# A recurrence with a mixture of experts behind it on one core: moving shared half units out of the recurrence, pairing reciprocal roots on VectorE, and two banks in turn for the later units

## The reference, cut to what matters

```python
# layer 1
xn = layernorm(x, ln_w, ln_b)
u = xn @ Ws.T + bs + xn @ Wi.T + bi          # 16 states
h_t = tanh(h_{t-1} @ A.T + u_t)              # 256 steps in order
out = (H @ Wo.T + bo) * sigmoid(xn @ Wg.T + bg) + x
x = layernorm(x + out)
# layer 2, T = 8192 tokens, E = 8 experts, top 2 of them
scores = softmax(x @ gate_w.T)
idx = top_k(scores + gate_b, 2); rw = scores at idx
h = silu((x @ w1 + b1) * (x @ w3 + b3))      # per expert, width 176
y = sum over the two experts of rw * (h @ w2 + b2)
z = the same with one shared expert for all tokens
x = layernorm(x + y + z)
```

## Time and profile before

| What | us |
|---|---|
| median of three runs | 517.06 |
| lowest, highest | 516.9, 523.76 |
| the profiled execution | 517.55 |
| its span (first to last instruction) | 515.8 |

### The profile page before, as it was taken

How to read it: one execution, slowest core, us unless ns; L and a number is a source line. 1 busy time by engine, 2 the same in 40 slices (tenths; PEclk the granted TensorE clock), 3 DMA queues, 4 the chain that set the end, 5 groups by cost and what they waited for, 6 DMA issues and landing times.

```text
span 515.8 us, 11180 instructions
## 1 busy us (share of the span) xinstructions
PE 451.1 (87%) x2842; PEld 353.6 (69%) x2842; DVE 347.0 (67%) x1562; ACT 336.7 (65%) x870; POOL 302.0 (59%) x331
## 2 busy tenths in 40 slices
PE   5879999999999988877898996899999998988691
PEld 3546766666666665666897875788888887777350
DVE  5454589898888989665757782345544568778772
ACT  3645777777777775464575764557677777777454
POOL 4100003777776775575677777777666577777232
PEclk9978999999999999799998998889999999999886
DMA  3663112333333222596465675567666588882472
GB/s 111 132 230 113 54 37 84 97 95 99 93 93 95 77 80 74 151 259 193 135 177 145 182 204 165 159 197 215 208 182 197 176 268 251 285 283 84 163 245 102
DMA packets 58228, 79.81 MB, mean 155 GB/s; under 512 B 11182, under 2 KB 37803, under 8 KB 58166
## 3 DMA queue, kind: packets, MB, share of 16 engines
q1 hardware_dynamic: 49516, 62.17, 41.7%
q0 software_dynamic: 8640, 16.93, 9.5%
q10 hardware_dynamic: 10, 0.00, 0.0%
HBM read 47.85 MB, written 25.84 MB: 143 GB/s over the span
## 4 chain that ended last, share of the span: by engine, by line
PE 48%; DVE 20%; issue 10%; POOL 9%; ACT 8%; SPq 2%; DMA 2%; ACTq 0%; DVEq 0%; POOLq 0%
PE py L1292 7%; PE p L1275 6%; PE py L1293 5%; PE pu L1347 5%; PE p L1280 5%; PE ph L1285 5%; POOL ys L585 4%; POOL xs L578 4%; PE pt L1429 2%; DVE z L1083 2%; PE pm L1406 2%; ACT hT L659 2%; DVE z L1078 2%; PE pu L1234 2%; ACT t3b L643 1%
## 5 line engine op out<-in xcount | busy, mean ns | idle before, releaser
L585 POOL DMA_INDIRECT ys<-yp,xp x142 | 145.0, 1021 | 58.6 <-issue 36.0
L578 POOL DMA_INDIRECT xs<-x,place_i x128 | 124.7, 974 | 58.9 <-issue 22.7
L659 ACT ACTIVATE hT<-pu,bu 16x32 f32<-16x32 f32 x256 | 78.7, 308 | 61.3 <-PE pu L1347 56.2
L650 ACT ACTIVATE hid<-z 128x512 f32<-128x512 f32 x103 | 64.7, 628 | 65.8 <-DVE z L1083 65.2
L1347 PEld LDWEIGHTS pu<-hT,aT 128*66 128x66 f32 x512 | 54.4, 141 | 58.0 <-ACT hT L659 52.9
L1347 PE MATMUL pu<-hT,aT 128*66 128x32 f32 x512 | 78.6, 241 | 11.9 <-ACT hT L659 11.7
L1078 DVE SCALAR_TENSOR_TENSOR z<-p,wp,t3a 128x256 f32<-128x256 f32 x71 | 34.3, 483 | 61.1 <-ACT t3a L638 54.5
L1292 PE MATMUL py<-wp,hid 128*128 128x128 f32 x284 | 59.2, 290 | 12.4 <-DVE yp L1104 9.7
L1292 PEld LDWEIGHTS py<-wp,hid 128*128 128x128 f32 x284 | 45.0, 192 | 27.9 <-DVE yp L1104 19.5
L1293 PE MATMUL py<-wp,hid 128*128 128x128 f32 x284 | 55.4, 277 | 0.0
L566 POOL TENSOR_TENSOR rstd_in<-ve_in,neghalf 128x4 f32<-128x4 f32 x16 | 16.4, 1027 | 66.3 <-DVE ve_in L793 66.2
(11 more groups left out here) (272 smaller groups left out, 969.7 us busy)
## 6 DMA issues: line engine op xcount, KB each, us to landing
wp<-packed SPq DMA_DIRECT2D x71, 320.0 KB, 3.4
xp<-xs SPq DMA_DIRECT2D x71, 130.0 KB, 2.9
weights<-ys SPq DMA_DIRECT2D x16, 512.0 KB, 4.7
xt<-in_L_attn_x SPq DMA_DIRECT2D x16, 256.0 KB, 3.1
x<-x SPq DMA_DIRECT2D x16, 256.0 KB, 2.7
packed<-weights SPq DMA_DIRECT2D x1, 2560.0 KB, 8.6
ys<-yp,xp POOLq DMA_INDIRECT x142
yb<-x SPq DMA_DIRECT2D x16, 128.0 KB, 2.7
```

The lines of the kernel that those rows point to most:

```text
L578: g.indirect_dma_start(out=xs[:, :], out_offset=bass.IndirectOffsetOnAxis(ap=place_i[b % NB][:, c, t * Q + q:t * Q + q + 1], axis=0), in_= ...
L585: g.indirect_dma_start(out=ys[:, :], out_offset=bass.IndirectOffsetOnAxis(ap=xp[j % NX][:, h, DEST:DEST + 1].bitcast(int32), axis=0), in_= ...
L650: nc.scalar.activation(hid[u % NH][:, :], z[u % 2][:, :], ACT.Silu).then_inc(hid_ready, 1)
L659: nc.scalar.activation(hT[k % 2][0:N, c], pu[k % 2][0:N, c], ACT.Tanh, bias=bu[:, 0:1]).then_inc(h_ready, 1)
```

## The change

The first halves of tiles 8 to 12 no longer run in the recurrence: `KEPT` = 8 tiles keep theirs there, and tiles 8 to 15 have both halves among the dense units, one shared half after every two pages (`BETWEEN` = 2) instead of three. For these tiles the transposed halves are kept in `yb` of the tile, and the DMA into `yb` is not made; both halves of the result take the tile's own rows from `x1`. At the places in the recurrence where the five units had their up and down matmuls (`w3a`, `w1a`, `wb`, `down`, `down_too`), TensorE does four dummy matmuls each, ahead of the step's own matmul.

The input roots of tiles 4 to 15 ride with the middle roots of the tiles four earlier: the two share buffers (`ve_two`, `rstd_two`), and the Newton instructions work on 8 values instead of 4. The input statistics lie three places later. GpSimd keeps the input roots of tiles 0 to 3.

Units from place 280 (`SWITCH`) to the last page use, in turn, `p1`, `p3`, `py` and, as second banks, `pu0`, `pu1`, `pm`; `ph` and `pt` stay single.

By the layout's rules the dense units are then 71 pages and 24 halves, places 250 to 344, the sums start 7 places later (`SUM_AT` of tile 0 goes from 319 to 326), and the whole count ends at 385 instead of 378.

```diff
-    AT = dict(load=-56, in_stats=-44, in_rstd=-42, ...
+    AT = dict(load=-56, in_stats=-41, in_rstd=-38, ...
+    SWITCH = 280
-    APART, FILL, AFTER, BETWEEN = 0, 0, 3, 3
+    KEPT, AFTER, BETWEEN = 8, 3, 2
     def lay_out_units():
-        start = {at("shared", k): ("shared", k, 0) for k in range(TILES) if at("shared", k) < PAGES_FROM - 8}
-        kept = [("shared", k, 1) for k in range(TILES)]
-        kept += [("shared", k, 0) for k in range(TILES) if ("shared", k, 0) not in start.values()]
...
+        start = {at("shared", k): ("shared", k, 0) for k in range(KEPT)}
+        kept = [("shared", k, 1) for k in range(KEPT)]
+        kept += [("shared", k, h) for k in range(KEPT, TILES) for h in range(HALF)]
...
+    TWO_BANKS = [u for u, unit in enumerate(UNITS) if SWITCH <= unit[0] <= UNITS[UNIT_OF_PAGE[sum(PAGES) - 1]][0]]
+    SECOND = set(TWO_BANKS[1::2])
+    def before_in_bank(u):
+        return max([v for v in range(u) if (v in SECOND) == (u in SECOND)], default=-1)
...
+        ve_two, rstd_two = ([sb(f"{w}_two{i}", [P, 2, Q]) for i in range(2)] for w in ("ve", "rstd"))
+    p1s, p3s, pys = (p1, pu[0]), (p3, pu[1]), (py, pm)
+        def of_unit(banks, u):
+            return banks[u in SECOND]
...
         def on_pool(w, turn):
-            return turn - SOON if w == "out" else turn
+            return turn - SOON if w == "out" else turn if turn < LEAD else -1
         def x1T_half(k, h):
+            if k >= KEPT:
+                return yb[k][:, h * HALF:(h + 1) * HALF, :].rearrange("p q d -> p (q d)")
+        QUIET = {at("shared", k) + SPARSE[what] for k in range(KEPT, TILES) for what in ("w3a", "w1a", "wb", "down", "down_too")}
+        QUIET = {n for n in QUIET if n < PAGES_FROM}
...
-                    if k >= APART:
+                    if k < KEPT:
                         sp.dma_start(yb[k][:, HALF:Q, :], x1_rows(k, 0)[:, HALF:Q, :]).then_inc(half_kept[k % NE], 16)
...
-                if k is not None:
+                if k is not None and k < LEAD:
                     rsqrt("in", k)
...
             def newton(w, k, part):
+                two = w == "mid" and k + LEAD < TILES
+                if two:
+                    y, ve_ = (t[i][:, :, :].rearrange("p n q -> p (n q)") for t in (rstd_two, ve_two))
...
+                    if two:
+                        v.wait_ge(ve_ready["in"], k + LEAD + 1)
+                        v.wait_ge(normed["in"], k + LEAD - NORMS["in"] + 1)
...
             def up_w3(u):
-                wait(pe, t3a_ready, u)
-                nc.tensor.matmul(p3[:, 0:PAGE], ...
+                bank_left(u)
+                wait(pe, t3a_ready, before_in_bank(u) + 1)
+                nc.tensor.matmul(of_unit(p3s, u)[:, 0:PAGE], ...
             def up_w1(u):
-                wait(pe, za_ready, u)
+                wait(pe, za_ready, before_in_bank(u) + 1)
             def down(u, h):
-                wait(pe, evacuated, u)
+                wait(pe, evacuated, before_in_bank(u) + 1)
...
             for n in range(BEGIN, END):
                 if n < first_down:
                     hold_clock(IDLE.get(n, 0) if n < 0 else 2 if n < 16 else 1)
+                if n in QUIET:
+                    pe.wait_ge(za_ready, KEPT)
+                    hold_clock(4, p1)
```

More of the change, by code:

```diff
@@ L110, in lay_out_units @@
     def lay_out_units():
-        start = {at("shared", k): ("shared", k, 0) for k in range(TILES) if at("shared", k) < PAGES_FROM - 8}
-        kept = [("shared", k, 1) for k in range(TILES)]
-        kept += [("shared", k, 0) for k in range(TILES) if ("shared", k, 0) not in start.values()]
-        for i, unit in enumerate(kept[:FILL]):
-            start[PAGES_FROM - FILL + i] = unit
-        among, behind = kept[FILL:len(kept) - AFTER], kept[len(kept) - AFTER:]
+        start = {at("shared", k): ("shared", k, 0) for k in range(KEPT)}
+        kept = [("shared", k, 1) for k in range(KEPT)]
+        kept += [("shared", k, h) for k in range(KEPT, TILES) for h in range(HALF)]
+        among, behind = kept[:len(kept) - AFTER], kept[len(kept) - AFTER:]
         n = PAGES_FROM
@@ L260, in rnn_gate_moe_block @@
         primer = sb("primer", [P, Q])
[L261 removed]
+        root_a, root_b = ({w: sb(f"root_{c}_{w}", [P, 2 * Q]) for w in ("mid", "out")} for c in "ab")
         tri_f, tri = sb("tri_f", [P, P]), sb("tri", [P, P], bf16)
@@ L292, in rnn_gate_moe_block @@
         x1 = sb("x1", [P, NE * 2 * Q, ROW])
-        x1T = [[sb(f"x1T{h}_{i}", [D, PAGE]) for i in range(n)] for h, n in enumerate((NS, TILES))]
+        x1T = [[sb(f"x1T{h}_{i}", [D, PAGE]) for i in range(n)] for h, n in enumerate((NS, KEPT))]
         yb = [sb(f"yb{k}", [P, Q, D]) for k in range(TILES)]
@@ L298, in rnn_gate_moe_block @@
         mv = {w: [sb(f"mv_{w}{i}", [P, Q, 2]) for i in range(NORMS[w])] for w in NORMS}
-        ve = {w: [sb(f"ve_{w}{i}", [P, Q]) for i in range(NORMS[w])] for w in NORMS}
-        rstd = {w: [sb(f"rstd_{w}{i}", [P, Q]) for i in range(NORMS[w])] for w in NORMS}
+        ve_two, rstd_two = ([sb(f"{w}_two{i}", [P, 2, Q]) for i in range(2)] for w in ("ve", "rstd"))
+        ve, rstd = ({"mid": [t[:, 0, :] for t in two], "in": [t[:, 1, :] for t in two],
+                     "out": [sb(f"{w}_out{i}", [P, Q]) for i in range(NORMS["out"])]} for w, two in (("ve", ve_two), ("rstd", rstd_two)))
         shift = {w: [sb(f"shift_{w}{i}", [P, Q]) for i in range(NORMS[w])] for w in NORMS}
@@ L682, in _ @@
                         act.wait_ge(x1T_ps, k + 1)
-                        if k >= NS and h == 0:
+                        if NS <= k < KEPT and h == 0:
                             act.wait_ge(lg_ps, k - NS + 1)
@@ L797, in scale @@
                 i = turn % NORMS[w]
-                if on_pool(w, turn) < 0:
+                if on_pool(w, turn) < 0 and w == "in":
+                    v.wait_ge(root_step["mid"], ROOT * (turn - LEAD + 1))
+                elif on_pool(w, turn) < 0:
                     v.wait_ge(root_step[w], ROOT * (turn + 1))
@@ L807, in newton @@
                 i = k % NORMS[w]
-                y, ve_, a, b = rstd[w][i][:, :], ve[w][i][:, :], root_a[w][:, :], root_b[w][:, :]
+                two = w == "mid" and k + LEAD < TILES
+                if two:
+                    y, ve_ = (t[i][:, :, :].rearrange("p n q -> p (n q)") for t in (rstd_two, ve_two))
+                else:
+                    y, ve_ = rstd[w][i][:, :], ve[w][i][:, :]
+                a, b = (t[w][:, 0:2 * Q if two else Q] for t in (root_a, root_b))
                 def then(step):
@@ L1093, in result @@
                     qs = slice(half * HALF, (half + 1) * HALF)
-                    if half == 1 and k >= APART:
-                        v.wait_ge(half_kept[k % NE], 16 * kept_of(k))
+                    if half == 1 and k < KEPT:
+                        v.wait_ge(half_kept[k % NE], 16)
                         own = yb[k][:, qs, :]
@@ L1262, in unit_of, with bank_left @@
                 return wp[a % NW][:, :], xpT[a % NP][:, :]
+            def bank_left(u):
+                if u == min(SECOND):
+                    pe.wait_ge(v_ready, TILES)
+                    pe.wait_ge(lg_ready, TILES)
+                    pe.wait_ge(x1T_ready, TILES)
+                    pe.wait_ge(place_ready, len(GROUPS))
+                    pe.wait_ge(table_step, TABLE + 1)
             def up_w3(u):
@@ L1314, in late_bank_free, with hold_clock @@
                 wait(pe, place_ready, sum(routed("rank", b) < n for b in range(len(GROUPS))))
-            def hold_clock(times):
+            def hold_clock(times, bank=py):
                 for _ in range(times):
-                    nc.tensor.matmul(py[:, 0:PAGE], ones[:, :], ones[:, :].unsqueeze(1).to_broadcast([P, HALF, P]), start=True, stop=True)
+                    nc.tensor.matmul(bank[:, 0:PAGE], ones[:, :], ones[:, :].unsqueeze(1).to_broadcast([P, HALF, P]), start=True, stop=True)
             def last_sum(k):
```

29 lines of the change are left out of this document (12 added, 17 removed).

## The result

| Four runs each | us |
|---|---|
| before: median (lowest, highest) | 517.03 (516.9, 523.76) |
| after: median (lowest, highest) | 536.27 (533.97, 539.07) |
| ratio, 95% interval | 1.0362 (1.0327 to 1.0397) |
| profiled execution after, its span | 533.97, 532.2 |

The changed kernel is 3.6% slower. The forecast was 521.6 with a range to 529. The profiled execution is the fastest of the four, so its trace shows 16.4 us of span more, and the median is another 2.3 above it. The slower executions have the lower clock: TensorE's mean granted clock is 0.940 in the fastest, then 0.934, 0.933 and 0.924 in the slowest; in the profiled execution of the kernel before it is 0.955.

What follows compares the result with a forecast made beforehand. It took the step chain, then GpSimd's scatters, then the ScalarE-VectorE loop as bounds. 1.0 - 6.3 - 2.3 + 12.1 + 0 = +4.5 us on the profiled 517.55 gave 522.05, 521.6 as a median; range 511 to 529.

Steps and rivals of the forecast that it cites:

- The recurrence: 256-step chain: dummy matmuls cost 3.8 us, VectorE's relief gives back 2.8; net +1.0 us, bounds -3 to +4.
- VectorE's stalls: TensorE's waits for a late VectorE in tiles 11 to 14, 2.8 us, were all taken as gone.
- The input roots: Moving 12 of 16 input roots from GpSimd to wider VectorE instructions changes nothing: 0, bounds -1 to +1 us.
- GpSimd's stretch: Scatter stretch from 249.48 to 332 us: two pages fewer, -5.1 us, and an earlier start, -1.2; in all -6.3.
- I take the middle, -1.2: The start of GpSimd's stretch could move by -3.6 to +1.2 us; -1.2 was taken.
- rival 3: Beginning of the pages costs more: page 2 waits for the transposer, no refill saving or VectorE relief; 529 us, chance 0.15.
- The refill: After VectorE's wait for a scatter at 335.99 us, a second bank brings the next `hid` sooner: -2.3 us, once.
- the steady loop: Dense units after the refill: the banks give nothing, periods stay 2.52 and 2.25 us.
- Rival 1: The banks shorten the dense units' loop to 2.41 and 2.19 us: -10.1 us, 511.5 us in all, chance 0.15.
- More units: Behind place 284, three more pages and two more halves cost +12.1 us; one normalizing pair fewer among the units, -1.5.
- Rival 4: The moved units cost nothing, hidden under GpSimd's work: 514.8 us; chance 0.2 together with another rival.
- The sums: Sums at the end: -1.5 us inside the units, +1.5 in the tail, 0 in total; bounds -2 to +3.

Runs made afterwards that it cites:

- e8: The changed kernel without the dummy matmuls that stand in for the moved units; 540.32 us, ratio 1.0407 to the kernel before.
- e9: The changed kernel with eight dummy matmuls in each place instead of four; 537.27 us, ratio 1.0369 to the kernel before.
- e7: The kernel before with the input-root change alone; 519.28 us, ratio 1.0027.
- e16: The changed kernel with shared halves at places 253, 256 and every third place on; 529.43 us, ratio 1.0207 to the kernel before.
- e6: The kernel before with the two banks alone; 515.40 us, ratio 0.9951.
- e18: The kernel before with shared halves at places 253, 257 and then every third place, one set of banks; 511.92 us, ratio 0.9881.
- e11: The kernel before with the two banks and shared halves at places 253, 257 and then every third place; 506.52 us, ratio 0.9794.
- e5: The changed kernel with shared halves at places 253, 257 and every third place from 260 on; 528.29 us, ratio 1.0226 to the kernel before.
- e3: The kernel before with the two banks alone, on a slow chip; 629.78 us against 626.80 for the kernel before there.
- e15: The kernel of e11 with shared halves at 253, 257 and every second place from 259 on; 508.50 us, ratio 0.9853 to the kernel before.

## Why the prediction was wrong

Three steps failed: that the granted clock stays as it is, that GpSimd has no pause once it has begun its stretch, and that the end of the program keeps its order.

**The recurrence (+1.0).** The step of the prediction that failed here is one that it doesn't name: it took TensorE's granted clock as unchanged. Its two terms were right where the clock was full. Four dummies against none make the step behind the logits 0.43 us longer (1.44 in the changed kernel, 1.01 in e8; forecast 0.44) and the step behind the transposes of `og` 0.31 (1.02 and 0.71; forecast 0.31); against the kernel before the first is 0.63 us longer (1.43 and 0.80), and what the other 0.2 are isn't known.

VectorE's stalls went as forecast: the waits for `og` of 0.38 and 1.31 us are gone in every kernel with moved units. In tiles 10 to 14 the steps that have no dummies take 45.2 us before and 42.2 in e9 at a clock of 1.00, but 45.5 in the changed kernel: so the clock costs 3.3 us there, and at the full clock the tiles would have taken about 63.8 us for the 64.1 before (an estimate: the 42.2 of e9 and the changed kernel's own 21.6 for the steps with dummies). The twelve steps from 239 to 251 take 13.4 us, against 11.1 in e9 and 11.0 before. So the units that left had done more than delay the chain; they had kept the clock up, and four dummies per place are too few: 0.93 and 0.74 instead of 1.00 and 0.87. (The edit also puts them at places 248 and 249, which I didn't count; the two steps take 0.4 us more.) Step 251 comes at 221.7 to 227.1 us in the four profiles with four dummies (mean 223.5) and at 214.7 to 217.9 in the six without moved units (mean 216.1). The term is +7.4 over these, +4.8 in the pair compared, and above my bound of +4 in both.

**The input roots (0).** e7 has +1.4 (0.1 to 2.7) where my bound was +1. Its profile reaches step 251 no later than the kernel before (215.8 and 217.1), so the recurrence doesn't lose it; where it is lost stays open.

**GpSimd's stretch (-6.3).** Two pages less are 5.1 us, and with the halves at 253 and 257 the stretch is 75.6 us instead of 81.2. In the changed kernel it is 78.7. The step that failed is the assumption that GpSimd has no pause once it has begun: it waits 3.31 us inside, for a page that slipped at a held place, and does so at any clock. "I take the middle, -1.2" for its start failed as well, with +1.6 from step 251; but that goes with the low clock and not with the held places, for e9, in the same order with the clock held, starts 1.4 earlier than before. I had page 2's wait for the transposer in view (rival 3), as one late unit of 2.3 us: by e16 place 253 has 3.2. Page 5 at place 257, which I did not look at, has 2.3 more in the profiles.

**The refill (-2.3), the steady loop (0).** The loop is right, by the periods. The refill is right for the order of the kernel before (e6: 2.0 us from the last routed scatter to place 287, 2.5 by the ratio). In the order of one half per two pages the banks have little left to save: e18 and e11 differ by 0.3 us there. The Trainium skill advises to rotate PSUM banks, so that the evacuation of one group overlaps the next (page "Perfetto Trace Analysis", section "Matmuls"); by that the loop would have become shorter. The trace disagrees here: `hid` still waits 0.62 us for `z` with either bank, since an in-order queue on ScalarE and not a bank holds the loop. Rival 1 is out. (Its sum, 26 x 0.09 and 28 x 0.12, doesn't follow from its own periods; 13 halves x 0.06 and 48 pages x 0.11 would be 6.1 for 5.7.)

**More units (+12.1, less 1.5).** Right: 10.8 measured for 10.6. Rival 4 is out.

**The sums (0).** The tail was to grow by 1.5 and grew by 6.2. I counted that sums start 7 places later and units end 5 later, but not that the seventh place is page 2's lag: all down projections from there on stand four places behind their unit, not three. So two units' downs (488.11 and 489.80 us) lie between the last `hid` and the first fold, in e5 one, before none. e5 and e16, without the lag, have 40.2 us: +0.8. Not all of the 5.4 us between is the lag, though. e9 has it too, at a full clock, and its end is 42.9; the other 2.7 go with the clock at which the last downs and the first folds run, after and e9:

```profile
486.00:500.00 14.00, 11.14 (x34) 7.10 (x34) 11.01 (x63) 3.92 (x9) 3.94 (x4) 0.76 0.44 135
```

```profile
486.00:500.00 14.00, 9.00 (x40) 5.56 (x38) 12.88 (x72) 5.33 (x13) 5.40 (x6) 1.00 0.54 184
```

e8, with the lag and a clock of 0.66 in the like stretch (493 to 503 us), has 45.4. Why the clock falls there in some profiles stays open.

With the halves at the right places, e5's profile has +6.4, -10.8, +10.6, +0.8 against my +1.0, -8.6, +10.6, +1.5. So two things were missed: the held places, 7 to 8 us of the median, and the clock with its dummies, 4 to 7 us. Rival 3 came nearest, its place right and its price too small; it left out the tail, and it looked for the loss in the recurrence in VectorE's stalls and not in the clock. How the recurrence would run with the units moved and the clock held at no cost isn't settled, since each run that held it paid in dummies.

## What to carry to other kernels

A stage order with held resources is not changed by a ratio: before one unit per two is placed where one per three was, list which places are held and what falls on them, and follow each slipped stage through TensorE's order to the end of the program. Work that fills the gaps of a latency chain also holds TensorE's clock; dummies that replace it must be counted as time and as clock. And a gain found inside a change that loses may be had alone: here the places of the shared halves and the second banks need none of the moved units, and gave 2.1%.

## What the runs showed of the hardware

The granted clock fell in a stage where TensorE looked busy for 89% of the time (25.00 of 28 us at 0.93, 186 matmuls) and stayed at 1.00 at 91 and 92% (e9 with 213 matmuls, the kernel before with 181 longer ones). Neither column alone warns of it: a matmul at the lower level is longer, so a slow engine looks busy.

Chips differ more than changes do. On two of the six chips that the experiments ran on, the kernel before took 627 and 628 us instead of 517. In e3's profile, on one of them, instructions last as long as elsewhere (`hid` 628 ns in both), but engines wait for something that the trace puts outside the core, as ScalarE for a page's transposes:

```profile
423.15 0.38 ACT L711 ACTIVATE xpT<-pt 128x256 f32<-128x256 f32 x1 [1.27 <-remote]
```

What that is stays open. The moved units hardly showed there (1.0087 for the kernel of e16, 1.0207 elsewhere), nor did the better places (0.9958 for that of e15, 0.9853 elsewhere), and the banks alone, a gain elsewhere (0.9951), were none (1.0051).
